# A place of its own for two weight blocks, a full float32 gate in the last chunk, and two multiplications moved towards the end

## The chip, the core and the metric

The kernel runs on one core of one Trainium2 chip. The metric is the device time of one execution in microseconds. The engines are TensorE (PE in the profile, its weight loads PEld), VectorE (DVE), ScalarE (ACT), GpSimd (POOL) and SyncE (SP), whose queue issues all the DMA transfers of this kernel. Each engine runs its own instructions in program order and waits on semaphores for the others.

## What is computed

The input is x with 128 rows of 512 and a context of 2048 rows of 512. Three residual steps follow each other. Cut to what matters:

```python
x = x + attention(layernorm(x), ctx)        # 32 query heads, 8 key/value heads
x = x + mamba2(layernorm(x))                # below
x = x + layernorm(x) @ w.T + bias           # w = scale * (digits - zero), 4-bit digits, 512x512

def mamba2(h):                              # INTER = 8192 = 128 heads of 64
    gate, hBC, dt = split(h @ in_proj_w.T)
    hs, B, C = split(silu(conv4(hBC)))      # B and C: 8 groups of 128
    dt = softplus(dt + dt_bias); X = hs * dt
    y = (C B^T * decay(dt, A)) X + D * hs   # one chunk of 128 positions
    xg = y * silu(gate)                     # then a norm over each group of 1024 columns
    return normed(xg) * norm_weight @ out_proj_w.T
```

The layer norm is (x - mean) / sqrt(var + eps) over a row. Everything is float32.

## The kernel before

Attention comes first, one key/value head after the other, with products in the float32r type. To keep precision there, an operand is split into a high part (a copy rounded to float32r) and a low part (the rest), and one product becomes three matmuls: high by high, low by high, high by low. That is the function `pairs`, lines 389 to 391. Making a high part is ScalarE's work, a low part is made by VectorE or, for the large weights, by GpSimd.

The Mamba stage works in 16 chunks c of 512 columns; chunk c is written 2n + i, and its slot in a ring of two buffers is i. Its order is written out by hand in each engine's function (`chunk_step` for TensorE, `chunk_act`, `chunk_dve`, `chunk_pool`), unrolled for n = 0 and n = 7 and a loop for 1 to 6. For a chunk TensorE does this:

- `hs_step` for the next chunk: 16 float32 matmuls of 128 columns (line 608), then four turns of hs (line 659)
- the gate: twelve `pairs` matmuls of 512 columns with w_gate_hi, w_gate_lo, xnT_hi and xnT_lo (line 675)
- the y matmuls: eight of 64 columns (line 687), into bank 4. They need x_dt and x_skip of VectorE (`x_ready`), the decay products (`m_ready`) and that `ygT_low` of the chunk before has read bank 4 (`ygT_lo_ready`)
- `out_step` of the chunk before (lines 639 to 652), with w_out_hi and w_out_lo; in the last group it is cut into two halves of 256 columns
- four turns of the gated y (line 696) once VectorE has made it (`y_gated`)

Where TensorE would stand idle at an end of the loop, it turns an identity matrix some times (`turn_identity`, line 396).

VectorE makes x_dt and x_skip from the turned hs (lines 1354 and 1356), the convolution of the next chunk (line 1337), the sum y + D hs (line 1365) and its product with the gate (line 1371), the decay of the next chunk (lines 1291 and 1299), the low part of the turned y (`ygT_low`, line 1324) and, in every second chunk, the addition of a finished group to xres (`add_group`, line 1344). In chunk 15 there is no next chunk, and in the convolution's place it multiplies the 4-bit weights by their scales (`scale_weights`, line 1314, four instructions). ScalarE makes the high parts and the silu; GpSimd makes w_out_lo (line 1481) and w_gate_lo (line 1486) and the small powers for the norms.

Before the loop TensorE projects B and C with four blocks of weights w_bc, each 1 MB (line 615). Blocks 0 and 1 are loaded into w_gate_sb, blocks 2 and 3 into w_out_sb; so the first weights of the gate and of the output are loaded only after these blocks have been read. SyncE's queue issues them in the order of lines 329 to 357. Buffers of the Mamba stage lie over those of attention, in the order in which they are named.

After the loop the last half group is added to xres, and the third layer norm follows: BN_STATS and BN_AGGR on VectorE, variance plus epsilon and the power -0.5 on GpSimd (`norm_scale`, lines 1419 and 1421), xn = (xres - mean) * rstd on VectorE (line 1013), four turns (line 403), ScalarE's copy xnT (line 997), eight float32 matmuls of 256 columns in two halves (line 736), the additions (line 1410) and the store.

## Time and profile before

| what | value |
|---|---|
| timed runs, median (lowest to highest), 3 runs | 716.35 us (713.92 to 716.79) |
| the profiled execution, its own time | 712.92 us |
| span of that execution on the core | 711.2 us |
| granted TensorE clock, mean | 1.00 of full speed |
| busy: PE, PEld, DVE, ACT, POOL | 697.0, 592.6, 549.5, 395.2, 300.5 us |
| attention, from the start to | about 486 us |
| Mamba: projections before the loop | about 487 to 511 us |
| Mamba: the 16 chunks | about 511 to 700 us |
| last layer norm and projection | about 700 to 711 us |

The span is the time between the first and the last instruction of the profiled execution; 1.72 us of its time lie around it. The timed runs were made without the profiler, and their median is 3.43 us above the profiled one. An engine's busy share says how much work it has, not that it bounds the kernel: a wait counts only if the chain of work that ends last passes through it. Matmuls overlap in the records, so the spacing of their starts tells their cost better than the length of one record.

### The profile page before, as it was taken

Reading aid. Unit: us, or ns where it says so; the run is one execution under the profiler, and the core shown is the slowest. Engines: PE = TensorE matmul, PEld = TensorE weight load, DVE = VectorE, ACT = ScalarE, POOL = GpSimd, SP = SyncE. Lnnn points to the kernel's source line nnn. Section 1 sums busy time; section 2 is a strip of 40 time slices with the busy share of each in tenths; the row PEclk is TensorE's granted clock in tenths of the full one; section 3 lists DMA queues with packets and bytes.
Section 4 is the critical chain, followed back from the end, with each engine's and each line's share of the span. In section 5 each row is a group of like instructions: output and inputs, shape, how many; then the busy total and the mean of one; then the engine's idle time right before and its main releaser. Section 6 shows DMA issues by size and latency. Waiting matters only on the chain.

```text
span 711.2 us, 12231 instructions
## 1 busy us (share of the span) xinstructions
PE 697.0 (98%) x4085; PEld 592.6 (83%) x4085; DVE 549.5 (77%) x1175; ACT 395.2 (56%) x603; POOL 300.5 (42%) x151
## 2 busy tenths in 40 slices
PE   8999999999999999999999999999999999999986
PEld 7888888888888888888888888879989999999975
DVE  5988578658748857866865874767999999999994
ACT  4563454535546446345553654654867667676752
POOL 2353223404504503331340440200388887888780
DMA  8702022021001102202102100832887878788600
GB/s 310 271 30 75 1 74 74 0 74 59 15 22 59 66 0 74 74 0 74 64 9 74 59 0 0 348 157 79 338 292 285 339 301 340 298 336 301 282 7 16
DMA packets 20293, 93.77 MB, mean 132 GB/s; under 512 B 2608, under 2 KB 3760, under 8 KB 11440
## 3 DMA queue, kind: packets, MB, share of 16 engines
q1 hardware_dynamic: 20272, 93.50, 35.5%
q8 instruction: 12, 0.20, 0.1%
q14 instruction: 9, 0.07, 0.0%
HBM read 93.17 MB, written 0.33 MB: 131 GB/s over the span
## 4 chain that ended last, share of the span: by engine, by line
PE 91%; DVE 4%; DMA 3%; issue 1%; ACT 1%; SPq 0%; POOLq 0%; POOL 0%; DVEq 0%
PE bank L389 24%; PE bank L391 22%; PE bank L390 22%; PE bank L608 10%; PE bank L516 5%; PE bank L687 3%; DMA w_hs_sb<-in_w_hs 1%; DMA wqo_raw<-in_wq 1%; PE bank L487 1%; PE bank L396 1%; DVE decay L1291 1%; PE bank L443 1%; PE bank L696 1%; PE bank L659 1%; PE bank L736 1%
## 5 line engine op out<-in xcount | busy, mean ns | idle before, releaser
L1448 POOL TENSOR_TENSOR wqo_lo<-wqo_raw,wqo_hi 128x2048 fp32r<-128x2048 f32 x15 | 69.6, 4640 | 192.3 <-ACT wqo_hi L744 163.6
L1121 DVE TENSOR_TENSOR pt_lo<-bank,pt_hi 128x512 fp32r<-128x512 f32 x128 | 87.6, 689 | 51.6 <-ACT pt_hi L818 50.8
L818 ACT ACTIVATE pt_hi<-bank 128x512 fp32r<-128x512 f32 x128 | 75.6, 597 | 57.0 <-PE bank L516 57.0
L1435 POOL TENSOR_TENSOR k_lo<-rope_a,k_hi 128x512 fp32r<-128x512 f32 x32 | 42.8, 1338 | 104.2 <-ACT k_hi L762 104.2
L1082 DVE CUSTOM_DVE_ANT_0 probs<-bank,mask_sb 128x512 f32<-128x512 f32 x128 | 82.0, 686 | 0.1
L1481 POOL TENSOR_TENSOR w_out_lo<-w_out_sb,w_out_hi 128x2048 fp32r<-128x2048 f32 x16 | 73.5, 4591 | 16.2 <-ACT w_out_hi L931 16.2
L1486 POOL TENSOR_TENSOR w_gate_lo<-w_gate_sb,w_gate_hi 128x2048 fp32r<-128x2048 f32 x15 | 69.3, 4618 | 18.0 <-ACT w_gate_hi L923 18.0
L516 PEld LDWEIGHTS bank<-ident_r,probs_r 128*128 128x128 f32 x512 | 55.8, 140 | 19.2 <-DVE pt_lo L1121 5.1
L808 ACT ACTIVATE probs<-probs,neg_max 128x2048 f32<-128x2048 f32 x31 | 61.9, 2001 | 0.9 <-DVE neg_max L1072 0.8
L608 PE MATMUL bank<-xnT,w_hs_sb 128*128 128x128 f32 x512 | 60.6, 277 | 1.0 <-DMA w_hs_sb<-in_w_hs 1.0
L516 PE MATMUL bank<-ident_r,probs_r 128*128 128x128 f32 x512 | 57.8, 238 | 1.5 <-DVE pt_lo L1121 1.5
L608 PEld LDWEIGHTS bank<-xnT,w_hs_sb 128*128 128x128 f32 x512 | 58.3, 192 | 1.1 <-DMA w_hs_sb<-in_w_hs 1.1
L389 PE MATMUL bank<-pt_hi,v_hi 128*128 128x512 f32 x128 | 57.8, 451 | 0.0
L1337 DVE SCALAR_TENSOR_TENSOR conv<-bank,cw,conv 128x127 f32<-128x127 f32 (+2 forms) x192 | 53.6, 341 | 5.4 <-DVE conv L1337 1.8
L762 ACT ACTIVATE k_hi<-rope_a 128x512 fp32r<-128x512 f32 x32 | 20.2, 633 | 60.6 <-DVE rope_a L1033 60.6
L389 PE MATMUL bank<-ctx_hi,wv_hi 128*128 128x512 f32 x128 | 51.3, 400 | 0.0
L389 PE MATMUL bank<-k_hi,qT_hi 128*128 128x512 f32 x128 | 51.2, 400 | 0.0
L389 PE MATMUL bank<-ctx_hi,wk_hi 128*128 128x512 f32 x128 | 50.9, 398 | 0.0
L391 PE MATMUL bank<-pt_hi,v_lo 128*128 128x512 f32 x128 | 50.5, 395 | 0.0
L390 PE MATMUL bank<-pt_lo,v_hi 128*128 128x512 f32 x128 | 50.3, 393 | 0.0
L391 PE MATMUL bank<-ctx_hi,wv_lo 128*128 128x512 f32 x128 | 50.1, 392 | 0.0
L391 PE MATMUL bank<-ctx_hi,wk_lo 128*128 128x512 f32 x128 | 50.0, 391 | 0.0
(193 smaller groups left out, 1728.2 us busy)
## 6 DMA issues: line engine op xcount, KB each, us to landing
w_hs_sb<-in_w_hs SPq DMA_DIRECT2D x16, 1024.0 KB, 4.8
w_gate_sb<-in_w_gate SPq DMA_DIRECT2D x16, 1024.0 KB, 4.8
w_out_sb<-in_w_out SPq DMA_DIRECT2D x16, 1024.0 KB, 6.3
wqo_raw<-in_wq SPq DMA_DIRECT2D x8, 1024.0 KB, 4.7
wqo_raw<-in_wo SPq DMA_DIRECT2D x8, 1024.0 KB, 4.8
decay<-decay_rows SPq DMA_DIRECT2D x16, 512.0 KB, 6.8
ctx_raw<-in_ctx_t SPq DMA_DIRECT2D x3, 1024.0 KB, 11.2
wk_raw<-in_wk SPq DMA_DIRECT2D x8, 256.0 KB, 2.7
```

What stands on the lines that cost most here:

```text
L389: pe.matmul(dst, left_hi, right_hi, start=first, stop=False)
L390: pe.matmul(dst, left_hi, right_lo, start=False, stop=False)
L391: return pe.matmul(dst, left_lo, right_hi, start=False, stop=last)
L516: last = pe.transpose(ring_b[(t + 1) % 2][:, h * P:(h + 1) * P].bitcast(F32R), probs_r[:, h, t * P:(t + 1) * P], ident_r[:, :])
L608: last = pe.matmul(dst[:, t * P:(t + 1) * P], w[:, c, t * P:(t + 1) * P], xnT[:, c, :], start=c == 0, stop=c == KC - 1)
L808: act.activation(probs[:, h, :], probs[:, h, :], ACT.Exp, bias=neg_max[:, h:h + 1], accum_out=row_sum[:, h:h + 1]).then_inc(s["probs_ready ...
L818: act.activation(pt_hi[t % 3], ring_b[(t + 1) % 2][:, :], ACT.Copy).then_inc(s["pt_hi_ready"], 1)
L1082: dve.tensor_tensor_reduce(out=probs[:, h, b * 512:(b + 1) * 512], in0=ring_a[b][:, :], in1=mask_sb[:, b * 512:(b + 1) * 512], scale=1.0, ...
L1121: dve.tensor_tensor(pt_lo[t % 3], ring_b[(t + 1) % 2][:, :], pt_hi[t % 3].bitcast(F32), ALU.subtract)\
L1448: pool.tensor_tensor(wqo_lo[:, :, :], wqo_raw[:, :, :], wqo_hi[:, :, :].bitcast(F32), ALU.subtract)\
L1481: pool.tensor_tensor(w_out_lo[:, i, :, :], w_out_sb[:, i, :, :], w_out_hi[:, i, :, :].bitcast(F32), ALU.subtract).then_inc(s["wout_lo_read ...
L1486: pool.tensor_tensor(w_gate_lo[:, i, :, :], w_gate_sb[:, i, :, :], w_gate_hi[:, :, :].bitcast(F32), ALU.subtract).then_inc(s["gate_lo_read ...
```

## The change

It has four parts.

Blocks 2 and 3 of w_bc get a buffer of their own, w_bc_sb, which lies at the addresses of w_out_lo, with semaphores of its own (`bc_in`). The first two w_out loads are then issued among the first loads, and blocks 2 and 3 after them, behind a wait for the last scores of attention.

In chunk 15 the gate is projected with four float32 matmuls from w_gate_sb and xnT instead of the twelve of `pairs`. ScalarE's `gate_high` and GpSimd's `gate_low` for that chunk are left out.

In chunks 14 and 15 VectorE's order changes: `ygT_low` and `add_group` of chunk 14 move behind x_dt and x_skip of chunk 15, and `scale_weights` moves from in front of the last sum to behind the last gated y.

In the third layer norm xn is xres - mean. The factor rstd is multiplied in with the two last additions, which become SCALAR_TENSOR_TENSOR instructions.

```diff
+        second_bc = ExitStack()
+        w_bc_sb = sb("w_bc_sb", [P, 2, KC, 512], F32, second_bc)
+        second_bc.close()
         w_out_lo = sb("w_out_lo", [P, 2, KC, 512], F32R, mam)
...
-            for i in range(BCC):
-                ring, sem = (w_gate_sb, gate_in) if i < 2 else (w_out_sb, wout_in)
-                sp.dma_start(ring[:, i % 2, :, :], w_bc[i]).then_inc(sem[i % 2], 16)
+            for i in range(2):
+                sp.dma_start(w_gate_sb[:, i, :, :], w_bc[i]).then_inc(gate_in[i], 16)
...
+            for i in range(2):
+                sp.dma_start(w_out_sb[:, i, :, :], w_out[i]).then_inc(wout_in[i], 16)
...
+            sp.wait_ge(s["scores_ready"], HG * KB * G)
+            for i in range(2):
+                sp.dma_start(w_bc_sb[:, i, :, :], w_bc[2 + i]).then_inc(bc_in[i], 16)
...
-            for i in range(2):
-                sp.wait_ge(s["bc_mm"], i + 3)
-                sp.dma_start(w_out_sb[:, i, :, :], w_out[i]).then_inc(wout_in[i], 16)
...
+                elif last_chunk:
+                    pe.wait_ge(gate_in[i], 16 * n + 32)
                 else:
                     pe.wait_ge(s["gate_lo_ready"], c)
...
+                    if last_chunk:
+                        last = pe.matmul(bank[2][:, :], xnT[:, k, :], w_gate_sb[:, i, k, :], start=k == 0,
+                                         stop=k == KC - 1)
...
-                    gate_high(n + i, 1 - i)
+                    if not (isinstance(n, int) and c == CH - 2):
+                        gate_high(n + i, 1 - i)
...
                 if last_chunk:
-                    scale_weights()
+                    ygT_low(n, 0)
+                    add_group(n - 1)
                 else:
                     conv_step(n + i, 1 - i)
...
-                if not last_chunk:
+                if last_chunk:
+                    scale_weights()
+                else:
                     scan_decay(n + i, 1 - i)
                     decay_products(n + i, 1 - i)
-                ygT_low(n, i, last_chunk)
-                if i == 0 and not first_group:
-                    add_group(n - 1)
+                if not next_to_last:
+                    ygT_low(n, i, last_chunk)
+                    if i == 0 and not first_group:
+                        add_group(n - 1)
...
+            dve.tensor_scalar(xn[:, :], xres[:, :], mean_var[:, 0:1], None, ALU.subtract).then_inc(s["xn_ready"], 1)
...
-                dve.tensor_tensor(xres[:, cols], xres[:, cols], src[:, 0:DM // 2], ALU.add)\
-                    .then_inc(s["ffn_added"], 1)
+                dve.scalar_tensor_tensor(xres[:, cols], src[:, 0:DM // 2], rstd[:, 0:1], xres[:, cols], ALU.mult,
+                                         ALU.add).then_inc(s["ffn_added"], 1)
...
-                gate_low(n + i, 1 - i)
+                if not (isinstance(n, int) and 2 * n + i == CH - 2):
+                    gate_low(n + i, 1 - i)
```

SyncE's queue in front of the Mamba loop, before. The rows ahead of these (not shown) include four w_bc loads, two into w_gate_sb and two into w_out_sb:

```order
L341 DMA w_hs_sb<-in_w_hs 128x2048
L342 DMA bias_bc<-in_q_bias 128x512
L343 DMA packed<-in_q_packed 128x1024
L344 DMA scale_sb<-in_q_scale 128x128
L345 DMA zero_sb<-in_q_zero 128x128
L348 DMA w_gate_sb<-in_w_gate 128x2048 x2
L350 DMA decay_rows<-step_decay 128x128
L326 DMA decay<-decay_rows 128x1024 x2
L357 DMA w_out_sb<-in_w_out 128x2048 x2
L372 DMA w_hs_sb<-in_w_hs 128x2048
```

The same stretch of SyncE's queue in the changed kernel, whose line numbers are shifted. Ahead of it stand only the two w_bc loads into w_gate_sb:

```order
L343 DMA w_hs_sb<-in_w_hs 128x2048
L345 DMA w_out_sb<-in_w_out 128x2048 x2
L346 DMA bias_bc<-in_q_bias 128x512
L347 DMA packed<-in_q_packed 128x1024
L348 DMA scale_sb<-in_q_scale 128x128
L349 DMA zero_sb<-in_q_zero 128x128
L352 DMA w_bc_sb<-in_w_bc 128x2048 x2
L355 DMA w_gate_sb<-in_w_gate 128x2048 x2
L357 DMA decay_rows<-step_decay 128x128
L329 DMA decay<-decay_rows 128x1024 x2
L376 DMA w_hs_sb<-in_w_hs 128x2048
```

The two w_out loads have moved from just ahead of the third w_hs load to the front of the series, and two w_bc loads have moved to its end.

VectorE's queue from the decay products of chunk 14 to the last turned y, before (bank 4 holds y and then the turned y, bank 6 the output of the group):

```order
L1299 TENSOR_TENSOR decay<-decay,bank5 128x512
L1324 SCALAR_TENSOR_TENSOR y_gT_lo<-bank4,nw,y_gT_hi 128x128 x4
L1344 SCALAR_TENSOR_TENSOR xres<-bank6,group_scale,xres 128x512
L1354 TENSOR_TENSOR x_dt<-bank3,dt 128x512
L1356 TENSOR_TENSOR x_skip<-bank3,d_bc 128x512
L1314 TENSOR_TENSOR weights<-weights,scale_sb 128x512 x4
L1365 TENSOR_TENSOR bank4<-bank4,x_skip 128x512
L1371 TENSOR_TENSOR y<-bank4,gate 128x512
L1324 SCALAR_TENSOR_TENSOR y_gT_lo<-bank4,nw,y_gT_hi 128x128 x2
```

And in the changed kernel:

```order
L1310 TENSOR_TENSOR decay<-decay,bank5 128x512
L1366 TENSOR_TENSOR x_dt<-bank3,dt 128x512
L1368 TENSOR_TENSOR x_skip<-bank3,d_bc 128x512
L1335 SCALAR_TENSOR_TENSOR y_gT_lo<-bank4,nw,y_gT_hi 128x128 x4
L1355 SCALAR_TENSOR_TENSOR xres<-bank6,group_scale,xres 128x512
L1378 TENSOR_TENSOR bank4<-bank4,x_skip 128x512
L1384 TENSOR_TENSOR y<-bank4,gate 128x512
L1325 TENSOR_TENSOR weights<-weights,scale_sb 128x512 x4
L1335 SCALAR_TENSOR_TENSOR y_gT_lo<-bank4,nw,y_gT_hi 128x128 x2
```

x_dt and x_skip of the last chunk have moved ahead of the low parts and the addition of chunk 14, and the four multiplications of the weights have moved from ahead of the last two y instructions to behind them.

## Rows read from the trace of the kernel before

**Rows 1.** Page, section 4: shares of the last-ending chain by engine

```profile
PE 91%; DVE 4%; DMA 3%; issue 1%; ACT 1%; SPq 0%; POOLq 0%; POOL 0%; DVEq 0%
```

**Rows 2.** Windows: length, busy PE, PEld, DVE, ACT, POOL, clock, DMA share, GB/s

```profile
536.00:548.00 12.00, 12.00 (x86) 10.91 (x85) 11.23 (x28) 8.47 (x15) 9.73 (x3) 1.00 0.80 299
...
680.00:692.00 12.00, 10.00 (x66) 8.81 (x65) 11.90 (x20) 6.83 (x11) 9.95 (x3) 1.00 0.01 1
```

**Rows 3.** Timeline, SyncE's queue: start, us, engine, line, operation

```profile
459.24 0.78 SPq L345 DMA_DIRECT2D zero_sb<-in_q_zero  x1
...
501.16 0.81 SPq L326 DMA_DIRECT2D decay<-decay_rows  x2
502.01 0.98 SPq L357 DMA_DIRECT2D w_out_sb<-in_w_out  x2
506.24 0.33 SPq L372 DMA_DIRECT2D w_hs_sb<-in_w_hs  x1
```

**Rows 4.** Page, section 6: DMA issues, KB each, median us to landing

```profile
w_hs_sb<-in_w_hs SPq DMA_DIRECT2D x16, 1024.0 KB, 4.8
```

**Rows 5.** Line 372 by itself (third w_hs load): us from issue to landing

```profile
DMA to landing us min/median/max: 9.3/9.3/9.3
```

**Rows 6.** Timeline, PE: start, us, work, in brackets idle time before and its releaser

```profile
495.32 7.31 PE L608 MATMUL bank<-xnT,w_out_sb 128*128 128x128 f32 x64
...
515.62 3.84 PE L608 MATMUL bank<-xnT,w_hs_sb 128*128 128x128 f32 x32 [0.98 <-DMA w_hs_sb<-in_w_hs]
```

**Rows 7.** Timeline, VectorE, start of the loop

```profile
517.42 3.41 DVE L1337 SCALAR_TENSOR_TENSOR conv<-bank,cw,conv 128x127 f32<-128x127 f32 x12
521.22 0.70 DVE L1365 TENSOR_TENSOR bank<-bank,x_skip 128x512 f32<-128x512 f32 x1 [0.40 <-PE bank L687]
```

**Rows 8.** Timeline, PE and its weight loads (PEld), the last chunk

```profile
686.81 0.50 PE L389 MATMUL bank<-w_gate_hi,xnT_hi 128*128 128x512 f32 x1 [2.00 <-POOL w_gate_lo L1486]
...
689.66 1.89 PE L687 MATMUL bank<-x_dt,decay 128*128 128x64 f32 x16
...
695.85 0.39 PEld L696 LDWEIGHTS bank<-ident_r,y_r 128*128 128x128 f32 x4 [0.30 <-DVE y L1371]
```

**Rows 9.** Timeline, VectorE, the last chunk

```profile
686.16 1.12 DVE L1324 SCALAR_TENSOR_TENSOR y_gT_lo<-bank,nw,y_gT_hi 128x128 fp32r<-128x128 f32 x4
687.20 0.74 DVE L1344 SCALAR_TENSOR_TENSOR xres<-bank,group_scale,xres 128x512 f32<-128x512 f32 x1
...
688.58 0.68 DVE L1356 TENSOR_TENSOR x_skip<-bank,d_bc 128x512 f32<-128x512 f32 x1
689.18 5.28 DVE L1314 TENSOR_TENSOR weights<-weights,scale_sb 128x512 f32<-128x512 f32 x4
694.38 0.68 DVE L1365 TENSOR_TENSOR bank<-bank,x_skip 128x512 f32<-128x512 f32 x1
...
697.09 1.13 DVE L1324 SCALAR_TENSOR_TENSOR y_gT_lo<-bank,nw,y_gT_hi 128x128 fp32r<-128x128 f32 x4 [1.30 <-ACT y_gT_hi L975]
```

**Rows 10.** Line 1314 by itself: duration ns min/median/max, starts

```profile
L1314 DVE TENSOR_TENSOR weights<-weights,scale_sb x4: 677/678/3472, 689.2 to 693.8; 128x512 f32<-128x512 f32 x4
```

**Rows 11.** Timeline, GpSimd, from the last chunk on

```profile
687.53 4.58 POOL L1481 TENSOR_TENSOR w_out_lo<-w_out_sb,w_out_hi 128x2048 fp32r<-128x2048 f32 x1 [0.77 <-ACT w_out_hi L931]
...
702.02 0.22 POOL L1419 TENSOR_SCALAR var_eps<-mean_var 128x1 f32<-128x1 f32 x1 [4.22 <-DVE mean_var L1011]
```

**Rows 12.** Timeline, VectorE, the last layer norm and additions

```profile
700.75 0.48 DVE L1397 SCALAR_TENSOR_TENSOR xres<-bank,group_scale,xres 128x256 f32<-128x256 f32 x1 [0.43 <-PE bank L391]
...
701.73 0.21 DVE L1011 BATCH_NORM_AGGREGATE mean_var<-stats 128x2 f32<-128x12 f32 x1
702.93 0.55 DVE L1013 TENSOR_SCALAR xn<-xres,mean_var,rstd 128x512 f32<-128x512 f32 x1 [1.00 <-POOL rstd L1421]
...
708.63 0.42 DVE L1410 TENSOR_TENSOR xres<-xres,bank 128x256 f32<-128x256 f32 x1 [1.24 <-PE bank L736]
```

**Rows 13.** Line 736 by itself (last projection): duration ns min/median/max, starts

```profile
L736 PE MATMUL bank<-wT,xnT x16: 379/379/483, 704.9 to 708.2; 128*128 128x256 f32 x16
```

More of the change, by code:

```diff
@@ L269, in build @@
         rope_k_in = [whole.enter_context(nc.semaphore(f"rope_k_in{b}")) for b in range(KB)]
-        gate_in, hs_in, wout_in, decay_in = ([s[f"{n}{i}"] for i in range(2)]
-                                             for n in ("gate_in", "hs_in", "wout_in", "decay_in"))
+        gate_in, hs_in, bc_in, wout_in, decay_in = ([s[f"{n}{i}"] for i in range(2)]
+                                                    for n in ("gate_in", "hs_in", "bc_in", "wout_in", "decay_in"))
         block = whole.enter_context(nc.Block())
@@ L674, in chunk_step @@
                 for k in range(KC):
-                    last = pairs(bank[2][:, :], xnT_hi[:, k, :], xnT_lo[:, k, :], w_gate_hi[:, k, :],
-                                 w_gate_lo[:, i, k, :], k == 0, k == KC - 1)
+                    if last_chunk:
+                        last = pe.matmul(bank[2][:, :], xnT[:, k, :], w_gate_sb[:, i, k, :], start=k == 0,
+                                         stop=k == KC - 1)
+                    else:
+                        last = pairs(bank[2][:, :], xnT_hi[:, k, :], xnT_lo[:, k, :], w_gate_hi[:, k, :],
+                                     w_gate_lo[:, i, k, :], k == 0, k == KC - 1)
                 last.then_inc(s["gate_mm"], 1)
@@ L1349, in chunk_dve @@
                 c = 2 * n + i
+                next_to_last = isinstance(n, int) and c == CH - 2
                 dve.wait_ge(s["hsT_mm"], c + 1)
```

12 lines of the change are left out of this document (8 added, 4 removed).

## Prediction

> **What bounds the kernel now.** I read the chain of work first: TensorE (PE) holds 91% of it [rows 1]. So a microsecond counts only where PE waits, or where a wait on another engine is handed to PE. The windows by stretch say where that is: in a steady stretch of the Mamba loop PE is busy for 12.00 of 12.00 us, at 680 to 692 us for 10.00 of 12.00 [rows 2]. Everything that the change moves lies at the loop's two ends, so I read the timelines of the queues there. Attention and chunks 2 to 13 keep their instructions, and I give them no change.
>
> I call the three places the start (506 to 530 us), the last chunk (684 to 698) and the tail (700 to 711). Times are those of the profiled execution, 712.92 us with a span of 711.2; the median of the timed runs is 716.35, 3.43 above it. I work out a saving on the former and take it off the latter.
>
> **The start.** Now SyncE issues two decay loads (512 KB each) at 501.16, two w_out loads (1 MB each) at 502.01 and w_hs of chunk 2 at 506.24 [rows 3]. The last takes 9.3 us to land [rows 5], where the median w_hs load takes 4.8 [rows 4]; PE waits 0.98 us for it and starts at 515.62 [rows 6]. The change gives the later B and C weights the place of w_out_lo, which nobody uses yet, so w_out is loaded with the first loads, before 465 us, and these 2 MB are gone from in front of w_hs. Even if w_hs still took 7 us it would land at 513.2, before PE is ready (515.62 - 0.98 = 514.64). I take the wait as gone: 0.98 us on PE.
>
> What is late next is VectorE. It runs the convolution of chunk 1 from 517.42 for 3.41 us, so it is free at 520.8, then idles 0.40 us and starts the sum of chunk 0 at 521.22, released by PE [rows 7]. With PE 0.98 us earlier the sum starts when VectorE is free, 0.40 us earlier, not 0.98. The chain then runs through VectorE until the loop settles, so 0.40 is what the loop inherits. Bounds: 0 (something else is late) and 0.98. The two loads that move are paid in a calm place: SyncE issues its last load of that series at 459.24 [rows 3], the two w_bc loads come right behind it, and PE starts on the third block of B and C weights at 495.32 [rows 6]. That wait stands in front of all later loads, but the first of those waits for bc_mm anyway. I put it at nothing; were they late, the wait would be what they take above 34 us.
>
> **The last chunk, gate.** PE has turned hs and waits 2.00 us for GpSimd's w_gate_lo, from 684.81 to 686.81; the twelve gate matmuls last until the y matmuls start at 689.66, so 2.85 us [rows 8]. Now four matmuls of full float32 over 512 columns take their place, with no low part to wait for. No such matmul of 512 columns with a 128-column weight is in the trace; the nearest are the eight of 256 columns in the last projection, each two records: 16 records start over 704.9 to 708.2 us, 15 steps of 0.22 us [rows 13]. Twice the columns give 0.44 us a record, and four matmuls are eight records: 3.5 us. I take that. Its bounds are 3.4 and 3.8 us. The gate would then end at 684.81 + 3.5 = 688.3, against 689.66: 1.35 us earlier, the 2.00 returned less 0.65 for the dearer form.
>
> **The last chunk, VectorE.** The y matmuls write the bank that ygT_low of chunk 14 reads, and wait for it and for x_dt and x_skip. Before, VectorE runs ygT_low at 686.16, the group's addition at 687.20, then x_dt, and x_skip at 688.58 [rows 9]. Now x_dt and x_skip come first, 0.61 us each (x_skip is followed at 689.18), then ygT_low, 1.12 us: 686.16 + 1.22 + 1.12 = 688.50. The y matmuls start at 688.55, set by VectorE and not by the gate, 1.1 us earlier than 689.66. The addition ends by 689.3, before PE reaches the output projection that wants its bank (some 1.7 us after 688.55).
>
> From there PE runs y, 24 output matmuls and 12 identity turns, and then turns y at 695.85; its weight loads wait 0.30 us for y before that [rows 8], so without y it would turn from 695.55 on. That wait comes from the scaling of the quantised weights, which holds the sum back to 694.38 [rows 9]. In the new order the sum follows the y matmuls at 688.55 + 1.9 = 690.5 and y ends at 691.9, early enough. PE turns y from 695.55 - 1.1 = 694.45 on if all of the 0.30 is real waiting, at 694.75 if none is: 1.1 to 1.4 us gained, and I take 1.3.
>
> **The scaling behind y** could take this back. Its four multiplications take 5.28 us [rows 9], and ygT_low of the last chunk now stands behind them. But one took 3472 ns and the others 677 or 678 [rows 10]: the first began at 689.18 and ended near 692.65, half a microsecond after GpSimd's w_out_lo ended at 687.53 + 4.58 = 692.11 [rows 11]. So it waited for GpSimd. In the new order it starts at 691.9, is released at the same 692.11 and the four end where they end now, at 694.46. First ygT_low is due at 697.09 - 1.3 = 695.8, when ScalarE has its high parts. The scaling is covered by 1.3 us; without cover it costs what it overruns. W_out_lo itself stays where it is, for its high part follows the turn of chunk 14, which doesn't move. I take 1.3 us for this place, bounds 0 and 1.7.
>
> The Trainium skill, SBUF — State Buffer, section Who interferes with whom, says that VectorE with two SBUF inputs and GpSimd reading SBUF exclude each other for a whole instruction; the long first multiplication agrees with it.
>
> **The tail.** BN_AGGR starts at 701.73 and lasts 0.21; xn starts at 702.93, having waited 1.00 us for rstd [rows 12]. Now xn only subtracts the mean, and 1/deviation is multiplied in with the last two additions. It can start at 701.97: 0.96 us. PE's sixteen turns of the weights and ScalarE's wT copies end just before the earlier xn needs them, which may keep 0.05. The last addition of 256 columns takes 0.42 us; the fused form of that size took 0.48 [rows 12], so 0.06 goes back. Sum 0.85 to 0.9. GpSimd has until 706 for rstd. Bounds: 0 and 1.0.
>
> The same section of the Trainium skill's page SBUF — State Buffer speaks against this step: a tensor_scalar may take, for a whole instruction, the ports that VectorE shares with GpSimd, and whoever issues first goes first. What a wait of xn for GpSimd would give is rival (b), worked out from rows.
>
> **Sum.** 0.4 + 1.3 + 0.9 = 2.6 us, 0.36% of 712.92. The profiled span would be 708.6 and the median 716.35 - 2.6 = 713.7.
>
> **Rivals.** (a) Every wait comes back in full: 0.98 + 2.00 + 1.00 = 4.0 us, 712.4. For it: they are all waits of the chain. Against it: VectorE's 520.8 and 688.50 come next at both places, and the gate is dearer.
>
> (b) VectorE waits for GpSimd. In the tail GpSimd starts the sum of variance and epsilon at 702.02 [rows 11], within 0.05 us of where xn would now start. If GpSimd goes first, xn waits at least its 0.22 us, and if the power that follows also goes first, xn gains nothing. At the last chunk, if the first multiplication stretches by 3.47 again wherever it stands, the scaling ends at 691.9 + 3.47 + 3 x 0.6 = 697.2 and the 1.3 us are gone too. Both: only 0.4 is left, 715.95; the tail alone: 1.7 us, 714.65. For it: the 3472 ns. Against it: the end of that stretch lies at GpSimd's end, and BN_AGGR's release on the same engine is quicker than the 0.08 us to GpSimd. By the rule of the Trainium skill, SBUF — State Buffer, Who interferes with whom, the tail hangs on these hundredths.
>
> (c) The start gives nothing, the rest as forecast: 2.2 us, 714.15.
>
> (d) Slower: the float32 gate takes twice my time, because a moving operand of 512 columns isn't two of 256. It would last 6.9 us, to 691.7, 2.05 us after today's 689.66. With 0.4 and 0.9 from the other places the kernel would be 0.75 us slower, 717.1. It decides against the change from a gate of about 6.2 us on. Against it: the 15 equal steps of the last projection [rows 13].
>
> **How the numbers follow.** Forecast 0.62, (a) 0.10, (b) 0.17, (c) 0.07, (d) 0.04. The likeliest gives 713.7. The savings of the cases that the range takes in run from 0.4 to 3.4 us (the upper bounds of the places after VectorE's limit: 0.7 + 1.7 + 1.0), 712.95 to 715.95. The timed runs lie between 713.92 and 716.79, so a median of other runs may stand 2 us lower or 0.5 higher: 711.0 to 716.4.
>
> About 0.5% (3.6 us) is what a measurement can tell from no change here. The forecast is below that, and only (a) is above. Faster by over 0.5%: (a) and a fifth to a quarter of the rest by measurement, 0.25. Slower by over 0.5%: no case by itself, 0.03 for what I don't see. Within: 0.72.
>
> **What would show it.** Start: no PE wait for w_hs, the sum of chunk 0 directly behind VectorE's convolution. Last chunk: no wait for w_gate_lo, eight gate records 0.44 us apart, the y matmuls released by ygT_low, the first weights multiplication short or under 1 us and the last over before the turned y's high part. Tail: xn directly behind BN_AGGR, 0.5 to 0.6 us long. I am wrong if the multiplications end after 695.8 on today's clock, if the gate lasts over 4 us, or if PE isn't full any more in the steady stretch.

## The result, and the profile after

| | before | changed |
|---|---|---|
| timed runs, median (lowest to highest), 7 runs each on one chip | 714.89 us (713.70 to 717.85) | 710.23 us (709.18 to 712.39) |
| the profiled execution, its own time | 712.92 us | 709.24 us |
| its span | 711.2 us | 707.5 us |
| granted TensorE clock of the profiled execution | 1.00 | 1.00 |

The ratio of the timed runs is put at 0.9939, with a 95% interval of 0.9916 to 0.9963; it is worked out from all runs, and the quotient of the two medians is 0.9935. The change makes the kernel 0.6% faster, where 0.36% was forecast, and 710.23 us lies below the range that I gave (711.0 to 716.4).

**The start.** PE, in the changed kernel: the third w_hs load is there, no wait stands in brackets.

```profile
513.47 3.81 PE L612 MATMUL bank<-xnT,w_hs_sb 128*128 128x128 f32 x32
```

VectorE behind it (convolution of chunk 1, sum of chunk 0), and then the third w_hs load by itself:

```profile
516.44 3.41 DVE L1348 SCALAR_TENSOR_TENSOR conv<-bank,cw,conv 128x127 f32<-128x127 f32 x12
519.77 0.69 DVE L1378 TENSOR_TENSOR bank<-bank,x_skip 128x512 f32<-128x512 f32 x1
```

```profile
DMA to landing us min/median/max: 4.7/4.7/4.7
```

The load takes 4.7 us instead of 9.3 [rows 5], and the sum stands directly behind the convolution.

**The last chunk.** PE, where the gate now is L682, the y matmuls L697, the turn of y L706:

```profile
683.19 3.67 PE L682 MATMUL bank<-w_gate_sb,xnT 128*128 128x512 f32 x8
...
687.17 1.97 PE L697 MATMUL bank<-x_dt,decay 128*128 128x64 f32 x16 [0.31 <-DVE y_gT_lo L1335]
...
693.13 0.54 PE L706 MATMUL bank<-ident_r,y_r 128*128 128x128 f32 x4
```

VectorE in the same place, the low parts of chunk 14 behind x_dt and x_skip, the scaling behind y:

```profile
684.71 0.68 DVE L1366 TENSOR_TENSOR x_dt<-bank,dt 128x512 f32<-128x512 f32 x1
685.31 0.68 DVE L1368 TENSOR_TENSOR x_skip<-bank,d_bc 128x512 f32<-128x512 f32 x1
685.91 1.11 DVE L1335 SCALAR_TENSOR_TENSOR y_gT_lo<-bank,nw,y_gT_hi 128x128 fp32r<-128x128 f32 x4
...
689.23 0.70 DVE L1378 TENSOR_TENSOR bank<-bank,x_skip 128x512 f32<-128x512 f32 x1 [1.55 <-issue]
689.97 0.69 DVE L1384 TENSOR_TENSOR y<-bank,gate 128x512 f32<-128x512 f32 x1
690.57 2.49 DVE L1325 TENSOR_TENSOR weights<-weights,scale_sb 128x512 f32<-128x512 f32 x4
694.37 1.13 DVE L1335 SCALAR_TENSOR_TENSOR y_gT_lo<-bank,nw,y_gT_hi 128x128 fp32r<-128x128 f32 x4 [1.31 <-ACT y_gT_hi L986]
```

GpSimd's low part of w_out, which held the first multiplication before [rows 10, 11], and the four multiplications by themselves:

```profile
686.07 4.56 POOL L1501 TENSOR_TENSOR w_out_lo<-w_out_sb,w_out_hi 128x2048 fp32r<-128x2048 f32 x1 [6.66 <-ACT w_out_hi L941]
```

```profile
L1325 DVE TENSOR_TENSOR weights<-weights,scale_sb x4: 683/684/687, 690.6 to 692.4; 128x512 f32<-128x512 f32 x4
```

The gate takes its eight records without a wait in front; the y matmuls wait 0.31 us for the low parts, as forecast; the four multiplications begin at 690.57, GpSimd is through at 690.63, and they are short (683 to 687 ns) and end 1.3 us before the next work of VectorE.

**The tail.** VectorE, then GpSimd:

```profile
698.99 0.21 DVE L1419 BATCH_NORM_AGGREGATE mean_var<-stats 128x2 f32<-128x12 f32 x1
699.24 0.49 DVE L1421 TENSOR_SCALAR xn<-xres,mean_var 128x512 f32<-128x512 f32 x1
...
704.88 0.48 DVE L1430 SCALAR_TENSOR_TENSOR xres<-bank,rstd,xres 128x256 f32<-128x256 f32 x1 [1.15 <-PE bank L746]
```

```profile
699.29 0.51 POOL L1439 TENSOR_SCALAR var_eps<-mean_var 128x1 f32<-128x1 f32 x1 [5.82 <-DVE mean_var L1419]
699.89 0.99 POOL L1441 TENSOR_TENSOR rstd<-var_eps,half_neg 128x1 f32<-128x1 f32 x1
```

xn stands directly behind BN_AGGR. GpSimd's two small instructions have grown from 0.22 us [rows 11] to 0.51 and from 0.57 to 0.99; nobody waits for them there.

**The two profiles side by side.** As a landmark I take the start of PE's turn of xn for the Mamba stage (line 403 before, 407 after), behind attention. Everything is counted from it:

| from the landmark, us | before | changed | gained so far | forecast |
|---|---|---|---|---|
| landmark itself, from the start | 485.73 | 484.74 | (0.99) | 0 |
| y of chunk 0 on VectorE | 36.23 | 35.75 | 0.48 | 0.40 |
| PE's y matmuls of chunk 15 | 203.93 | 202.43 | 1.50 | 1.5 |
| PE's turn of y of chunk 15 | 210.12 | 208.39 | 1.73 | 1.7 |
| xn of the third norm | 217.20 | 214.50 | 2.70 | 2.66 |
| end of the span | 225.5 | 222.8 | 2.7 | 2.6 |

So between these two executions every term of the sum holds. Two things don't follow from it: the 0.99 us in front of the landmark, and a median of all runs that fell by 4.66 us.

### The profile page after: what moved, and what is told of

Same layout as the page of the kernel before. It is cut to its first block and busy times, and to the rows that moved or that the text cites. A ratio compares the mean times of both kernels' runs of the same rounds, so it can differ in the third digit from the quotient of the medians.

```text
span 707.5 us, 12227 instructions
## 1 busy us (share of the span) xinstructions
PE 696.7 (98%) x4081; PEld 591.2 (84%) x4081; DVE 547.0 (77%) x1175; ACT 393.6 (56%) x602; POOL 297.4 (42%) x150
## 5 line engine op out<-in xcount | busy, mean ns | idle before, releaser
L1506 POOL TENSOR_TENSOR w_gate_lo<-w_gate_sb,w_gate_hi 128x2048 fp32r<-128x2048 f32 x14 | 64.7, 4619 | 16.7 <-ACT w_gate_hi L933 16.7
```

Of the source, the lines that this page charges most:

```text
L1506: pool.tensor_tensor(w_gate_lo[:, i, :, :], w_gate_sb[:, i, :, :], w_gate_hi[:, :, :].bitcast(F32), ALU.subtract).then_inc(s["gate_lo_read ...
```

## The experiments

Every kernel was timed together with the kernel before on the same chip. r1 to r4 share one set of runs of before (29 runs, median 715.29), r5 to r8 a second (30, 714.57), r9 to r11 a third (29, 715.37), r12 a fourth (17, 714.30). Each timed run also lists its span and its mean granted TensorE clock, and that is what the experiments turned on. In the table a run at 0.998, 0.997 or 0.995 is one whose clock fell for a few microseconds:

| kernel | median us | ratio to before (95%) | runs at clock 1.000 | their mean span | at 0.998 / 0.997 / 0.995 |
|---|---|---|---|---|---|
| before, all four sets | 714.3 to 715.4 | | 18 of 105 | 711.4 | 35 / 24 / 28 |
| changed, first runs | 710.23 | 0.9939 (0.9916 to 0.9963) | 7 of 7 | 708.6 | 0 / 0 / 0 |
| r2 changed, again | 710.63 | 0.9909 (0.9881 to 0.9936) | 6 of 6 | 708.9 | 0 / 0 / 0 |
| r8 changed, no identity turns | 709.10 | 0.9911 (0.9880 to 0.9942) | 7 of 7 | 707.2 | 0 / 0 / 0 |
| r1 before, again | 715.66 | 0.9985 (0.9963 to 1.0007) | 4 of 12 | 712.4 | 3 / 3 / 2 |
| r3 start alone | 713.99 | 0.9970 (0.9948 to 0.9992) | 2 of 12 | 710.6 | 6 / 4 / 0 |
| r4 tail alone | 714.76 | 0.9981 (0.9956 to 1.0006) | 2 of 12 | 709.9 | 8 / 1 / 1 |
| r6 gate alone | 714.76 | 1.0005 (0.9978 to 1.0031) | 5 of 12 | 711.6 | 1 / 3 / 3 |
| r7 VectorE's order alone | 713.86 | 0.9990 (0.9964 to 1.0017) | 5 of 12 | 710.5 | 5 / 1 / 1 |
| r12 last chunk alone (r6 and r7) | 713.08 | 0.9984 (0.9962 to 1.0006) | 8 of 12 | 710.6 | 2 / 1 / 1 |
| r9 changed, less the start | 712.10 | 0.9951 (0.9930 to 0.9971) | 10 of 12 | 709.9 | 2 / 0 / 0 |
| r10 changed, less the tail | 712.19 | 0.9952 (0.9932 to 0.9971) | 9 of 12 | 710.0 | 2 / 1 / 0 |
| r11 changed, scaling in front | 713.48 | 0.9964 (0.9946 to 0.9981) | 4 of 12 | 710.2 | 4 / 4 / 0 |
| r5 before, waits filled | 713.89 | 0.9978 (0.9957 to 0.9999) | 10 of 12 | 711.6 | 2 / 0 / 0 |

The four sets ran on four chips. The mean span of the kernel before at clock 1.000 was 710.9 us in the first, 711.6 in the second, 711.8 in the third and 710.9 in the fourth, from 3 to 6 runs each. So a difference of under 1 us between kernels of different sets can't be read from this table.

### Before and changed once more (r1, r2)

No edit in either.

> The kernel before, unchanged, under another name. I call the head of a profile the time up to TensorE's turn of the second normalised input (485.73 us in the profile before, 484.74 in the one after) and the rest of the span the body (225.5 us before, 222.8 after). Theory T: the 1.0 us by which the two heads differ is scatter of the first loads from execution to execution, since both kernels have the same instructions there. Then this kernel's head lies anywhere in 484.5 to 486.5 and its body is 225.5 +- 0.2; ratio 1.000 +- 0.002. Rival S: something fixed in the changed program makes the head 1.0 us shorter. Then this head is 485.7 +- 0.2 and the repeat of the changed kernel beside it 484.7 +- 0.2.

> The changed kernel once more. T: body 222.8 +- 0.2 and a ratio that belongs to the 2.7 us of the body, 0.9962, measured 0.994 to 0.998. S: head 484.7 again, ratio 0.9948 (3.7 us) in the middle. Rival M: the ratio first measured, 0.9939 or 4.4 us, is the change's own worth in undisturbed timed runs, and it comes again at 0.994.

r2 came out as none of the three views had it: its part behind the landmark is 222.7 us long, as expected, but its ratio of 0.9909 lies below all three. r1 missed the expected 225.5 us: its part behind the landmark is 229.3 us long. The profiled execution of the unchanged kernel was this time 714.2 us long, 3.0 more than the first one of the same program. Two of its stretches say why. PE's timeline at the start and in the tail:

```profile
516.92 3.84 PE L608 MATMUL bank<-xnT,w_hs_sb 128*128 128x128 f32 x32 [3.12 <-DMA w_hs_sb<-in_w_hs]
...
706.18 5.41 PE L736 MATMUL bank<-wT,xnT 128*128 128x256 f32 x16 [0.69 <-ACT xnT L997]
```

and the windows of the tail (the number before the DMA share is the granted clock):

```profile
706.00:708.00 2.00, 1.82 (x6) 1.48 (x7) 0.00 (x0) 0.13 (x1) 0.00 (x0) 0.68 0.00 0
708.00:710.00 2.00, 2.00 (x6) 1.62 (x5) 0.42 (x1) 0.00 (x0) 0.00 (x0) 0.50 0.00 0
```

First, the wait for w_hs is 3.12 us, not 0.98 [rows 6]. Second, the last projection takes 5.41 us instead of 3.72, because in its midst the clock is at 0.50 of full speed, that is 1.2 instead of 2.4 GHz. PE had waited 1.08 us for xn and 0.69 us for xnT just before. Neither is in the profile that I predicted from, though the same waits for xn and xnT are. PE in that first profile of the kernel before:

```profile
703.53 0.66 PE L403 MATMUL bank<-ident,xn 128*128 128x128 f32 x4 [1.08 <-DVE xn L1013]
...
704.87 3.72 PE L736 MATMUL bank<-wT,xnT 128*128 128x256 f32 x16 [0.69 <-ACT xnT L997]
```

**Why the w_hs wait differs.** SyncE's queue in this execution of the kernel before:

```profile
497.71 0.35 SPq L350 DMA_DIRECT2D decay_rows<-step_decay  x1
502.27 0.81 SPq L326 DMA_DIRECT2D decay<-decay_rows  x2
503.13 0.91 SPq L357 DMA_DIRECT2D w_out_sb<-in_w_out  x2
505.42 0.33 SPq L372 DMA_DIRECT2D w_hs_sb<-in_w_hs  x1
```

The store of the decay rows goes out at 497.71 and the loads that read it back only at 502.27, 4.56 us later. In the first profile that took 2.63 us (498.53 to 501.16 [rows 3]). Then the 2 MB of w_out are issued 2.3 us ahead of w_hs instead of 4.2, and w_hs lands 11.5 us after its issue. The eight profiles of kernels with the old order of loads fall into two groups: step of 2.4 to 2.6 us, landing 9.1 to 9.5, wait 0.71 to 1.16 (before, r4, r6, r7, r12); step of 4.56 to 4.90 us, landing 11.5 to 11.7, wait 2.38 to 3.19 (r1, r5, r9; in r5 PE had 1.17 us of other work ahead of its 2.38). That the late step makes the late landing is read from this pairing; no run changed the step alone. In the first profile of the changed kernel the step was as late as that too (4.71 us), and it didn't matter, since w_hs landed in 4.7 us:

```profile
497.55 0.35 SPq L357 DMA_DIRECT2D decay_rows<-step_decay  x1
502.26 0.81 SPq L329 DMA_DIRECT2D decay<-decay_rows  x2
505.25 0.33 SPq L376 DMA_DIRECT2D w_hs_sb<-in_w_hs  x1
```

The landmark was at 484.91 and 487.50 in these two executions, against 485.73 and 484.74 before. Over all 14 profiles it lies between 484.74 and 487.50, in no order by kernel. The 0.99 us ahead of the landmark is scatter and not an effect of the change; the parts behind it are 222.8 and 222.7 us long in the two executions of the changed kernel.

### One part alone (r3, r4)

r3 is the kernel before with w_bc_sb and the new order of SyncE's loads:

```diff
-            for i in range(BCC):
-                ring, sem = (w_gate_sb, gate_in) if i < 2 else (w_out_sb, wout_in)
-                sp.dma_start(ring[:, i % 2, :, :], w_bc[i]).then_inc(sem[i % 2], 16)
+            for i in range(2):
+                sp.dma_start(w_gate_sb[:, i, :, :], w_bc[i]).then_inc(gate_in[i], 16)
...
+            for i in range(2):
+                sp.dma_start(w_out_sb[:, i, :, :], w_out[i]).then_inc(wout_in[i], 16)
...
+                sp.dma_start(w_bc_sb[:, i, :, :], w_bc[2 + i]).then_inc(bc_in[i], 16)
```

r4 is the kernel before with the new third norm:

```diff
-            layer_norm(3)
+            dve.wait_ge(s["norm_stats"], 6)
+            dve.bn_aggr(mean_var[:, :], stats[:, :, :].rearrange("p a b -> p (a b)")).then_inc(s["norm_agg"], 1)
...
+            dve.tensor_scalar(xn[:, :], xres[:, :], mean_var[:, 0:1], None, ALU.subtract).then_inc(s["xn_ready"], 1)
...
+                dve.scalar_tensor_tensor(xres[:, cols], src[:, 0:DM // 2], rstd[:, 0:1], xres[:, cols], ALU.mult,
+                                         ALU.add).then_inc(s["ffn_added"], 1)
```

> Only the place for blocks 2 and 3 of the B and C weights and the earlier w_out loads; nothing else of the change. Forecast's step: the 0.98 us wait of TensorE for w_hs is gone, but VectorE's convolution is late next, so the body is 0.4 us shorter (225.1). Rival a: the whole 0.98 comes back (224.5). Rival c: nothing (225.5). Ratio by the forecast 0.9994, not to be told from 1.

> Only the last layer norm: xn without the deviation, which is multiplied in at the end. Forecast's step: 0.9 us (body 224.6), xn directly behind BN_AGGR and GpSimd's two small operations longer than before, since VectorE has the shared ports first. Rival b: xn waits for GpSimd and the gain is 0.7 or less (224.8 or more). T and S about the head as in the other runs.

r3: there is no w_hs wait, y of chunk 0 comes 35.74 us behind the landmark, like 35.75 in the changed kernel. But in the timed runs this part is worth more than the 0.4 us, "not to be told from 1", that I had expected: the ratio of 0.9970 keeps 1 out of its interval, and the mean span is 712.0 us against 714.0 for before in the same set. None of its 12 runs shows 0.995, of before's 105 runs 28 do. In its profile the clock fell in the tail again, and the projection took 5.41 us.

r4: xn stands directly behind BN_AGGR and takes 0.49 us, as in the whole change. The clock fell too, but in another place, behind the 2 us wait for w_gate_lo in the last chunk. PE there, and the windows:

```profile
687.26 0.80 PE L389 MATMUL bank<-w_gate_hi,xnT_hi 128*128 128x512 f32 x1 [1.99 <-POOL w_gate_lo L1490]
```

```profile
686.00:688.00 2.00, 0.74 (x2) 0.65 (x3) 2.00 (x7) 1.91 (x2) 1.22 (x2) 0.77 0.00 0
688.00:690.00 2.00, 2.00 (x7) 1.52 (x6) 1.97 (x4) 0.00 (x0) 2.00 (x1) 0.50 0.00 0
```

The twelve gate matmuls then last 4.35 us, not 2.85 [rows 8].

### The waits filled instead of removed (r5)

The kernel before, with more turns of the identity matrix where PE waits: sixteen ahead of the last gate (bank 2), nine ahead of the third hs projection (bank 4), nine and five around the turn of xn in the tail (bank 5).

```diff
+                elif last_chunk:
+                    at_least(pe, s["gate_act"], c)
+                    turn_identity(16, bank[2])
+                    pe.wait_ge(s["gate_lo_ready"], c)
...
+                    turn_identity(9, bank[4])
...
+            turn_identity(9, bank[5])
...
+            turn_identity(5, bank[5])
```

> The kernel before with nothing of the change, but with identity turns in four of TensorE's waits: 9 before the third hs projection, 16 before the last gate, 9 and 5 in the last layer norm. They compute nothing that is used and shorten no wait. Theory K: the kernel before loses some 2 us in most executions because after such waits the granted clock falls to half for some 4 us (29 runs beside the last ones: mean span 710.9 in 3 runs at a mean clock of 1.000, 712.9 to 713.3 in 16 runs at 0.997 or 0.998, 716.5 in 10 runs at 0.995), and the changed kernel was at 1.000 in all of its 13. Then this kernel is at 0.999 or 1.000 in nearly all runs and its median is 1.5 to 3 us under the kernel before, ratio 0.996 to 0.998. Rival W: the clock differs by chance or chip, and the time by the waits alone. Then the mixture of clocks is as before and the ratio is 1.000 or above by the turns that overlap nothing.

It keeps every late buffer of the kernel before and only gives PE something to do at three places. 10 of 12 runs are now at 1.000, against 6 of 30 for before in the same set, and the mean span is 712.2 against 713.4 us. At clock 1.000 nothing is gained (711.6 in both). That separates the clock from the waits: the awaited things come as late as ever, but the clock seldom falls behind the waits. The gain is smaller than I had expected, though: the median is 0.7 us lower and not 1.5 to 3. The sixteen turns leave 0.25 us of the wait for w_gate_lo; the nine turns at the start last 1.17 us, and where w_hs is late, as in this profile, they leave most of the wait empty. This is one of the two runs below 1.000, and its fall lies there (PE, then the windows behind the wait):

```profile
514.81 1.17 PE L396 MATMUL bank<-ident 128*128 128x128 f32 x9
518.37 5.47 PE L608 MATMUL bank<-xnT,w_hs_sb 128*128 128x128 f32 x32 [2.38 <-DMA w_hs_sb<-in_w_hs]
```

```profile
521.00:523.00 2.00, 2.00 (x12) 2.00 (x11) 0.18 (x1) 0.63 (x1) 2.00 (x1) 0.50 1.03 434
```

### The two halves of the last chunk (r6, r7, r12)

r6 is the kernel before with the float32 gate:

```diff
+                    if last_chunk:
+                        last = pe.matmul(bank[2][:, :], xnT[:, k, :], w_gate_sb[:, i, k, :], start=k == 0,
+                                         stop=k == KC - 1)
```

r7 is the kernel before with VectorE's new order, and r12 has both edits, with start and tail as before:

```diff
-                    scale_weights()
+                    ygT_low(n, 0)
+                    add_group(n - 1)
...
+                if last_chunk:
+                    scale_weights()
```

> Only the full float32 gate of the last chunk, with its high and low parts left out. Forecast's step: the 2.00 us wait is gone and the gate lasts 3.5 us, but the y matmuls then wait for VectorE's x_skip and the scaling still stands before the sum, so the y turn moves little: 0 to 0.3 us in the body at full clock. Theory K adds: no fall of the clock before the last chunk's gate any more, while the falls in the last layer norm stay, so 0.995 becomes rare and the median is 1 to 2 us lower. Rival W: ratio 0.9995 to 1.000 and clocks as before.

> Only VectorE's new order in the last two chunks; the gate keeps its twelve matmuls and waits for w_gate_lo. The gate then ends at about the same 689.6 as before and the y matmuls start there, but the sum follows them at once instead of at 694.38, and the turn of y waits only for TensorE's own matmuls: 0.2 to 0.3 us in the body at full clock, by the 0.30 that the weight loads waited for y. The scaling: its first multiplication long only as far as w_out_lo on GpSimd still runs. Clock falls as in the kernel before (K and W alike), since the 2.00 us wait stays.

> The kernel before with the changes of the last chunk alone, the float32 gate and VectorE's new order together; start and tail as before. By the sum of my prediction: 1.3 us less than the kernel before at the same clock, 1.26 us by the trace of the changed kernel (y turned 206.1 us behind attention's last turn of xn, where the kernel before takes 207.4 less what the w_hs wait differs). Each of the two halves alone moved the median by 0.0 and -0.1%. Theory C (the clock falls behind waits, and two of its places, w_hs and the tail, are left, the place in the last chunk is closed): timed runs at 1.000 have a mean span of 709.7 to 710.5, some are at 0.997 and 0.998, 0.995 at most once; median 712.5 to 713.8, ratio 0.995 to 0.998. Rival W (the waits' own length alone counts): ratio 0.998 with the clocks spread as in the kernel before, a third of the runs at 0.995.

r6, PE and VectorE: the gate ends early, but then PE waits for x_skip behind the old order, and the sum waits for the scaling as ever.

```profile
688.57 2.00 PE L693 MATMUL bank<-x_dt,decay 128*128 128x64 f32 x16 [1.00 <-DVE x_skip L1363]
```

```profile
688.43 5.23 DVE L1321 TENSOR_TENSOR weights<-weights,scale_sb 128x512 f32<-128x512 f32 x4
693.59 0.69 DVE L1372 TENSOR_TENSOR bank<-bank,x_skip 128x512 f32<-128x512 f32 x1
```

r7, VectorE: the scaling behind y takes 2.49 us, but the y matmuls stay behind the 1.99 us for w_gate_lo.

```profile
693.43 0.69 DVE L1373 TENSOR_TENSOR y<-bank,gate 128x512 f32<-128x512 f32 x1
694.04 2.49 DVE L1314 TENSOR_TENSOR weights<-weights,scale_sb 128x512 f32<-128x512 f32 x4
```

From the landmark to the turn of y, corrected by the w_hs wait of each execution: before 210.12, r6 0.04 less, r7 0.27 less, r12 1.26 less. The halves are worth 0.3 us apart and 1.26 us together, since each leaves the other's limit standing. In r12's 12 runs the ratio is 0.9984, outside the 0.995 to 0.998 that I had expected, and the interval takes in 1: the microsecond is seen in the trace, not in the timed runs. 0.995 came once, and 8 of 12 runs are at 1.000, against 3 of 17 for before beside it. r6 went against my view of the clock: with the wait for w_gate_lo gone I expected 0.995 to be rare and the median 1 to 2 us lower, but 0.995 came in 3 of 12 runs and the ratio is 1.0005. Its new wait of 1.00 us for x_skip is a possible reason, which no run tests. r7, which leaves all three waits, has as many runs at 1.000 as r6, 5 of 12.

### The changed kernel less one part (r9, r10, r11)

r9 is the changed kernel with r3's edit taken back, r10 with r4's taken back, and r11 with the scaling in front of the last sum:

```diff
+                    scale_weights()
...
-                if last_chunk:
-                    scale_weights()
-                else:
+                if not last_chunk:
```

> The changed kernel with its later B and C weights loaded into w_out_sb again, as before, so that the third w_hs load stands behind the two w_out loads and PE waits for it (0.7 to 3.1 us in the traces so far). Theory C (the granted clock falls behind a PE wait, and each part of the change took one such place away): one place is left, so some of the timed runs show a mean clock of 0.997 or 0.998, none 0.995; those at 1.000 have a mean span of 709.0 to 709.6 (0.4 above the changed kernel's 708.7), those below it are 2 to 3 us longer. Median 710.5 to 712, ratio to the kernel before 0.994 to 0.998. Rival W (only the waits themselves count, the clock is chance): the clock reads 1.000 or below as often as in the kernel before (9 of 59 runs at 1.000), whatever is left out. In the profile: y of chunk 0 some 0.4 us or more later against the landmark in attention; the last chunk and the tail as in the changed kernel.

> The changed kernel with the third layer norm as before (rstd multiplied into xn, plain additions). By the sum of my prediction it is 0.9 us longer than the changed kernel at the same clock: xn waits 1.00 us for rstd again, the last addition comes 0.9 us later against the turned y. Timed runs at clock 1.000: mean span 709.4 to 709.8. Theory C1: the clock falls in the tail because of the wait for rstd; then some runs are at 0.998. Theory C2: the waits of the tail alone (1 us, 0.7 us) do not make it fall when nothing went before them; then all runs are at 1.000, median 711.4, ratio to the kernel before 0.995.

> The changed kernel with the scaling of the weights in front of the last sum again. Forecast by the rows: the scaling waits for GpSimd's w_out_lo (ends about 690.6 on the changed kernel's times) and ends 1.9 us later, at 692.5 or 693, so the sum is made 3 us later than in the changed kernel (689.23) and y ends at about 694.3; PE turns y then instead of at 693.13 with its twelve identity turns in front: 0.9 to 1.4 us later. Median 1 to 1.4 us above the changed kernel's at the same clock (709.7 to 710.2 span). Rival: the identity turns and the 24 output matmuls cover it, 0.0 to 0.3 us. In either case the y matmuls start where they do in the changed kernel.

r9: one place is left, and, as expected, two of 12 runs are below 1.000, none at 0.995. The profiled one is such a run; PE, and the windows behind the wait:

```profile
518.10 5.18 PE L608 MATMUL bank<-xnT,w_hs_sb 128*128 128x128 f32 x32 [3.19 <-DMA w_hs_sb<-in_w_hs]
```

```profile
518.00:520.00 2.00, 1.90 (x9) 1.90 (x10) 1.95 (x8) 0.00 (x0) 2.00 (x2) 0.50 0.99 406
```

Its runs at 1.000 are 1.2 us above the changed kernel's 708.7, not 0.4 as I had put it. The w_hs wait, which is now 1 us and now 3, would account for it, but so would the chip for part: before's own runs at 1.000 are 711.8 in this set and 711.4 over all.

r10: three of 12 below 1.000, so the tail's waits alone are enough (the second of my two variants falls). xn waits 1.00 us for rstd, and then PE's last projection:

```profile
704.38 5.41 PE L746 MATMUL bank<-wT,xnT 128*128 128x256 f32 x16 [0.69 <-ACT xnT L1008]
```

Its runs at 1.000 are 1.3 us above the changed kernel's, where the sum has 0.9. Against before in the same set they are 1.8 us shorter (710.0 against 711.8), and the sum has 2.6 - 0.9 = 1.7 for that.

r11: VectorE, PE and the windows. The first multiplication again waits until GpSimd's w_out_lo is through (692.48), y is late, and PE, its twelve identity turns done, waits 0.99 us for it:

```profile
689.56 5.26 DVE L1325 TENSOR_TENSOR weights<-weights,scale_sb 128x512 f32<-128x512 f32 x4
```

```profile
696.22 0.54 PE L706 MATMUL bank<-ident_r,y_r 128*128 128x128 f32 x4 [0.99 <-DVE y L1385]
```

```profile
698.00:700.00 2.00, 2.00 (x11) 2.00 (x12) 0.59 (x3) 0.00 (x0) 0.17 (x1) 0.59 0.00 0
```

The turn of y comes 209.63 us behind the landmark, 1.24 later than in the changed kernel, as forecast from the rows, and the four runs at 1.000 have a mean span of 710.2, at the end of the 709.7 to 710.2 that I had put. But the median is 3 us higher, not 1.4: only 4 of 12 runs are at 1.000. Doing the multiplications in front makes a new empty place, followed by the 1.21 us in which PE waits for the low parts, and the clock falls behind that.

### Without the identity turns in the last chunk (r8)

```diff
-                if first or last_chunk:
-                    turn_identity(12, bank[1] if last_chunk else bank[3])
+                if first:
+                    turn_identity(12, bank[3])
```

> The changed kernel without the 12 identity turns between the output matmuls and the turn of y in the last chunk. In the changed kernel y is ready at 690.66 and is turned at 693.13, behind these turns, so they are on the path now (1.2 to 1.4 us); in the kernel before they filled a wait. VectorE's scaling ends at 693.06 and the first high parts would be there at about 692.9, so nothing else is late. At full clock the body is 1.2 us shorter than the changed kernel's. K warns: TensorE then stands idle for 1.2 us with less work before it, and if the clock falls behind that the 24 half matmuls and the turns at half clock cost 2 us or more, and the median is above the changed kernel's. W: 1.2 us in all runs.

Both kernels so far turn the identity matrix twelve times between the output matmuls and the turn of y; this one leaves that out. In the changed kernel y is ready before PE is, so PE's twelve turns of the identity matrix, 1.22 us, now stand on the path. Without them the turn of y comes directly behind the output matmuls, and VectorE's low parts directly behind the scaling (PE, then VectorE):

```profile
693.29 0.45 PE L706 MATMUL bank<-ident_r,y_r 128*128 128x128 f32 x4
```

```profile
691.97 2.49 DVE L1325 TENSOR_TENSOR weights<-weights,scale_sb 128x512 f32<-128x512 f32 x4
694.43 1.13 DVE L1335 SCALAR_TENSOR_TENSOR y_gT_lo<-bank,nw,y_gT_hi 128x128 fp32r<-128x128 f32 x4
```

From the landmark the turn of y comes at 207.15 us, 1.24 earlier than in the changed kernel; the part behind the landmark is 221.5 us long against 222.8. All seven runs stay at 1.000, and their mean span is 1.5 us below the 708.7 of the changed kernel's thirteen. This is the fastest version, 709.10 us, ahead of both kernels. It was not run side by side with the changed kernel in one set, so its lead over that rests on the two sets' spans and on the trace.

## Why the prediction was off

**The start: right in the profile, too small in the mean.** No wait for w_hs, the sum directly behind the convolution, 0.48 us against 0.40. The failed step is "so 0.40 is what the loop inherits": the 0.98 us [rows 6] was one draw of two. Where the decay rows come back late the wait is about 3.1 us (r1, r9) and y of chunk 0 comes 38.36 us behind the landmark (r1) instead of 36.23, and the same part of the change is then worth 2.6 us. The two later w_bc loads cost nothing, as said.

**The last chunk: right.** The gate's eight records take 3.67 us (forecast 3.5, bounds 3.4 to 3.8); the y matmuls start when ygT_low has ended and not when the gate has, 1.02 us earlier against y of chunk 0 than before (forecast 1.1); the turn of y gains 1.25 (forecast 1.3). Rival (d), a gate twice as long, is out. The measured 4.66 us lie nearest to rival (a), in which all waits come back in full for 4.0 us, but its mechanism isn't what happened: y of chunk 0 gained 0.48 us and not 0.98, the y matmuls 1.02 more and not 2.00.

**The scaling behind y: right.** It is covered. That the first multiplication waits for the end of GpSimd's instruction and isn't slow by itself is shown from both sides: in front of the sum the four take 5.23 and 5.26 us (r6, r11), behind y 2.49 (changed, r7, r8, r12). The rule of the Trainium skill, SBUF — State Buffer, section Who interferes with whom, that VectorE with two inputs in SBUF and GpSimd reading SBUF keep each other out, holds for these instructions.

**The tail: right.** xn goes 0.97 us earlier against the turn of y (forecast 0.96), the last addition keeps 0.48 us. Rival (b) is out: VectorE went first by 0.05 us in the changed kernel, in r4 xn didn't wait either, and GpSimd's instruction of 0.22 us took 0.51: it ended at 699.80, just behind xn's end at 699.73, as if it had waited for it. What xn does when GpSimd goes first, no execution here shows.

**The step from the profile to the median: wrong.** This is the step that put the forecast too high. I wrote "I work out a saving on the former and take it off the latter", with 3.43 us between the two that I didn't explain. They were not a constant. By the 105 runs of the kernel before, the mean span is 713.7 us, and that of the 18 runs at clock 1.000 is 711.4. The 28 runs at 0.995 have a mean of 716.4. The changed kernel's thirteen runs are all at 1.000, with a mean of 708.7. So at equal clock the change gives 711.4 - 708.7 = 2.7 us, near the sum of 2.6, and another 713.7 - 711.4 = 2.3 us come from runs in which the clock fell, or w_hs was later, and which the changed kernel doesn't have. That 2.7 and 2.6 lie so close is partly luck: before's spans at 1.000 go from 710.4 to 713.9, their mean differs by 1 us from set to set, and the timed runs don't tell which of them had the late w_hs. I had no rival in which the removed waits cost more than their length; the one profile of before stood at clock 1.00 throughout and couldn't show one, but its long idle places in front of matmuls, 0.98, 2.00 and 1.08 us, could be read.

**The base.** The three runs shown had a median of 716.35 us; seven gave 714.89, and the sets of 17 to 30 runs 714.3 to 715.4. Of the 3.5 us between 713.7 and 710.23, 1.5 are that, and I had allowed 2 for it; the other 2.1 (4.66 less 2.6) are what the step left out, the clock and the late w_hs; how they share it isn't shown. The range's low end held the first and had nothing for the second.

**How far the clock is shown.** Seven of 14 profiles have a fall, and each lies right behind an empty place of PE or at its end: the tail (r1, r3, r10), w_gate_lo (r4), w_hs (r5, r9), the late y (r11). Each costs 1.3 to 1.7 us. What shows the waits as the cause is the filler work of r5 (10 of 12 runs at 1.000 against 6 of 30), the opened place of r11 (4 of 12), and that with all three closed 20 of 20 runs are at 1.000. Closing one place alone isn't told from before by this count (r3 2, r4 2, r6 5 of 12). An estimate of the shares, if the places fall independently: with w_hs alone left 10 of 12 runs are whole (r9), with the tail alone 9 of 12 (r10), with both that makes 0.63 (r12 has 8 of 12); before has 0.17, so the wait for w_gate_lo would be passed without a fall in only about 0.17 / 0.63, a quarter of the runs, and be the costliest of the three. No run left it as the only place. The Trainium skill, TensorE: Matmul & The Clock Gate, section HAM oscillation — how this bites in real kernels, says that a wait between bursts of matmuls can throttle the clock so that the next burst starts slow; these rows agree, with 5.41 us for 3.72 us of matmuls. The DMA waits of its example, 3 to 5 us, are longer than the 1.0 to 3.2 us behind which it fell here.

Open is why one execution falls and the next, with the same waits, doesn't: the w_gate_lo wait was 2.00 us long in before and in r1 without a fall, and 1.99 in r4 with one. Open is also why the decay rows take 2.4 to 2.6 us in seven of the 14 profiles and 4.3 to 5.1 in the other seven. Not tried was a kernel without the trip of the decay rows through DRAM.

## What to carry to other kernels

Before a saving worked out in one profile is taken off a median, look at the clocks and spans of all timed runs: if the profile is at clock 1.000 and most runs aren't, each empty place of TensorE in front of matmuls can cost its length plus a share of the 1.3 to 1.7 us that a fall took here, and removing it is worth both. A wait for a load behind other loads should be read in more than one execution, since its length went here with the time at which a small store came back. And when a change makes the awaited thing early, the filler work that used to bridge the wait has to go as well; here it held 1.2 us.

## What the runs showed of the hardware that I had not expected

- The same program, with the same waits, has TensorE at 1.00 throughout in one execution and at 0.50 for a stretch in another: 0.5 for the whole window of 708 to 710 us in r1, with 0.68 and 0.96 in those beside it. That lowers the mean clock of a run of 714 us to 0.998. The kernels with one such place never showed 0.995 (r9, r10, r11, 36 runs).
- A small store to DRAM, up to the issue of the load that waits for it, took 2.4 to 2.6 us in seven of the 14 profiles and 4.3 to 5.1 in the other seven, with the same instructions in both. In the eight profiles with the old order of loads a 1 MB load behind it landed in 9.1 to 9.5 us or in 11.5 to 11.7 us accordingly.
- GpSimd's additions and powers on 128 values took 0.51 and 0.99 us beside VectorE's instructions on 512 columns, against 0.22 and 0.57 us with VectorE waiting.
